# The order of the two halves' feed-forward layers around the second per-position attention: half 0 first, half 1 between the relays

## The reference, cut to what matters

```python
x = _layernorm(x + _L0_attn_ref(x, ...))   # per token: 32 heads attend to each other's 16 dims
x = _layernorm(x + _L0_ffn_ref(x, ...))    # three dense layers with +-1 weights, relu between them
x = _layernorm(x + _L1_attn_ref(x, ...))   # rotary, causal attention in a window of 128 tokens, 32 heads
x = _layernorm(x + _L1_ffn_ref(x, ...))    # a shared expert and the best 2 of 16 experts
```

## Time and profile before

| | |
|---|---|
| median of 3 runs | 777.63 us (777.32 to 779.89) |
| the profiled execution's own time | 780.3 us |
| its span, first to last instruction | 778.5 us |
| busy in the span | PE 83%, PEld 65%, DVE 53%, ACT 33%, POOL 27% |
| mean granted TensorE clock | 0.881 of 2.4 GHz |

### The profile page before, as it was taken

One profiled execution on the slowest core, in us unless ns is written; L12 is line 12 of the kernel. 1 busy time (PEld: TensorE's weight loads), 2 busy tenths in 40 slices (PEclk: granted clock), 3 DMA queues, 4 the chain that ended last, 5 costly groups with the idle time before them and its releaser, 6 DMA issues.

```text
span 778.5 us, 16447 instructions
## 1 busy us (share of the span) xinstructions
PE 643.4 (83%) x6644; PEld 502.8 (65%) x6644; DVE 412.6 (53%) x1155; ACT 253.2 (33%) x412; POOL 208.4 (27%) x305
## 2 busy tenths in 40 slices
PE   3998998864878687698998989596579979999984
PEld 3886877753756565476675766474347868887761
DVE  3445454478556375574776748462547224332354
ACT  4243001733437223232443334254321012221213
POOL 4000000462010115343544445245103621110061
PEclk9997998767889997698999989675789989999997
DMA  8920002131100752725537254602002939998455
GB/s 301 384 91 4 3 3 88 32 86 30 48 0 26 191 132 46 152 83 83 133 48 151 81 86 128 129 4 83 1 0 89 370 109 404 393 417 326 177 166 184
DMA packets 45786, 102.40 MB, mean 132 GB/s; under 512 B 11088, under 2 KB 15312, under 8 KB 44176
## 3 DMA queue, kind: packets, MB, share of 16 engines
q1 hardware_dynamic: 28528, 62.73, 22.6%
q0 software_dynamic: 12720, 30.50, 17.4%
q10 hardware_dynamic: 4464, 8.13, 2.8%
HBM read 63.77 MB, written 35.13 MB: 127 GB/s over the span
## 4 chain that ended last, share of the span: by engine, by line
PE 56%; DMA 12%; DVE 11%; issue 7%; ACT 6%; POOL 6%; SPq 1%; POOLq 0%; ACTq 0%; DVEq 0%
PE bank L317 15%; PE bank L353 10%; PE bank L526 10%; ACT FP L1487 3%; PE bank L594 3%; DVE FP L923 3%; DMA slots_out<-FP 3%; PE bank L609 3%; DMA QS<-QS 2%; PE bank L581 2%; POOL slots_in L1819 2%; DMA QS<-slots_out 2%; POOL FP L1831 2%; PE bank L729 2%; DVE W L923 2%
## 5 line engine op out<-in xcount | busy, mean ns | idle before, releaser
L1487 ACT ACTIVATE FP<-bank 128x512 f32<-128x512 f32 (+1 forms) x246 | 140.8, 612 | 335.2 <-PE bank L594 133.7
L1216 DVE CUSTOM_DVE_ANT_0 kraw<-bank,maskb 128x256 bf16<-128x256 f32 (+1 forms) x256 | 88.5, 401 | 63.9 <-PE bank L581 63.9
L526 PE MATMUL bank<-W,XR 128*128 128x512 f32 x384 | 116.1, 450 | 0.1
L317 PE MATMUL bank<-FP 128*128 128x128 f32 x558 | 89.3, 315 | 1.6 <-ACT FP L1487 1.6
L526 PEld LDWEIGHTS bank<-W,XR 128*128 128x128 f32 x384 | 78.5, 216 | 18.1 <-DVE XR L923 0.7
L353 PE MATMUL bank<-W,XR 128*128 128x512 f32 x288 | 82.0, 432 | 4.8 <-DVE W L923 4.8
L1782 POOL TENSOR_SCALAR_AFFINE_SELECT FP<-FP 128x512 f32<-128x512 f32 x64 | 41.3, 669 | 114.3 <-ACT FP L1487 114.3
L353 PEld LDWEIGHTS bank<-W,XR 128*128 128x128 f32 x288 | 60.9, 235 | 14.2 <-DVE W L923 5.2
L317 PEld LDWEIGHTS bank<-FP 128*128 128x128 f32 x558 | 67.0, 196 | 3.7 <-issue 2.1
L317 PE MATMUL bank<-RP,W 128*128 128x512 f32 x224 | 54.9, 402 | 4.3 <-DVE FP L923 2.2
L317 PEld LDWEIGHTS bank<-RP,W 128*128 128x128 f32 x224 | 42.8, 193 | 14.7 <-issue 4.4
(11 more groups left out here) (162 smaller groups left out, 1029.5 us busy)
## 6 DMA issues: line engine op xcount, KB each, us to landing
FP<-in_experts_dram SPq DMA_DIRECT2D x31, 768.0 KB, 6.7
slots_out<-QS SPq DMA_DIRECT2D x48, 256.0 KB, 2.6
FP<-slots_in POOLq DMA_DIRECT2D x31, 256.0 KB, 6.5
slots_out<-FP ACTq DMA_DIRECT2D x31, 256.0 KB, 7.2
slots_in<-RP SPq DMA_DIRECT2D x7, 1024.0 KB, 9.0
RP<-slots_out POOLq DMA_DIRECT2D x16, 384.0 KB, 5.8
QS<-slots_out POOLq DMA_DIRECT2D x10, 384.0 KB, 8.9
FP<-in_shared_dram SPq DMA_DIRECT2D x4, 768.0 KB, 8.3
```

Of the source, the lines that this page charges most:

```text
L317: mm = nc.tensor.matmul(bank, lhs, rhs, start=(n == 0), stop=(n == len(terms) - 1))
L526: mm = nc.tensor.matmul(b[:, :], *terms[n], start=(n == 0), stop=(n == len(terms) - 1))
L1216: ins = nc.vector.tensor_tensor_reduce(masked[:, 2 * (f % 2) + m, 0:n], b[:, m, :], maskb[:, m0:m0 + n], 1.0, -BIG, ALU.add, ALU.max, hmax ...
L1487: return nc.scalar.activation(o, i, func, **kw)
```

## The change

On PE half 0's first hidden layer moves into steps c = 6 and 7 of the second core, ahead of `values_by_four(6)` and `(7)`. Its second layer and last layer follow with half 1's context transposes in front or between; tile 0's projections (key, query) come right behind, ahead of all of half 1's FFN; half 1's FFN is laid between tile 0's and tile 1's rotations and projections; its four `last_layer` calls move into the loop's pass i = -1. In step c = 0 half 0's normalisation moves from DVE (`normalise`) to DVE's `rates` and ACT's `normalise`. `ffn_out` gives tile 0's statistics by themselves, so tile 0's root, rates and normalisation have a batch of their own. These buffers become separate ones: `h1[0]`, `hf`, tile 0's x2 (`x2T`); the stack semaphores become two for each kind, by the parity of the tile. SP's load of the output weights (`ao`) goes behind tile 1's relays; ACT's split of them from step (-1, 3) to (0, 6), and POOL's subtraction for them from (0, 1) to (1, 0). The diff, cut to its core:

```diff
-        h1 = [RP[:, 0:4096].rearrange("p (a c n) -> p a c n", a=2, c=DC),
+        h1 = [QS[:, 0:4096].rearrange("p (a c n) -> p a c n", a=2, c=DC),
...
-        hf = FP[:, 16512:17536].rearrange("p (b n) -> p b n", b=2)
+        hf = [FP[:, a:a + 1024].rearrange("p (b n) -> p b n", b=2) for a in (14336, 16512)]
...
+        x2T = [QS[:, 0:1024].rearrange("p (a c n) -> p a c n", a=2, c=DC)] + [XT2[:, 0]] * (T - 1)
+        coT = XT2[:, 1]
...
                 if AHEAD <= c < AHEAD + G:
                     turn_x1(c - AHEAD)
+                elif c >= AHEAD + G:
+                    hidden(0, 0, *range(2 * (c - AHEAD - G), 2 * (c - AHEAD - G) + 2))
                 values_by_four(c)
...
-            hidden(0, 0, 0)
             contexts(1, 0, 1)
-            hidden(0, 0, 1)
-            contexts(1, 2)
-            hidden(0, 0, 2)
-            contexts(1, 3)
-            hidden(0, 0, 3)
-            hidden(0, 1, *range(DC))
+            hidden(0, 1, 0)
+            contexts(1, 2, 3)
+            hidden(0, 1, 1, 2, 3)
+            last_layer(0, 0, 1, 2)
+            turn_x(0)
+            last_layer(0, 3)
+            project2(0, 1)
             turn_x1(G)
             turn_x1(G + 1)
-            last_layer(0, 0, 1)
+            project2(0, 0)
             turn_x1(G + 2)
             turn_x1(G + 3)
-            last_layer(0, 2, 3)
-            hidden(1, 0, 0, 1, 2)
-            turn_x(0)
+            turn_rotated(0, 1)
+            hidden(1, 0, 0, 1)
+            turn_rotated(0, 0)
+            hidden(1, 0, 2)
+            turn_x(1)
             hidden(1, 0, 3)
-            project2(0, 1)
-            project2(0, 0)
+            project2(0, 2)
+            project2(1, 1)
             hidden(1, 1, 0)
-            turn_rotated(0, 1)
-            hidden(1, 1, 1)
-            turn_rotated(0, 0)
-            project2(0, 2)
-            hidden(1, 1, 2, 3)
-            turn_x(1)
-            last_layer(1, 0)
-            project2(1, 1)
+            project2(1, 0)
+            turn_rotated(1, 1)
+            hidden(1, 1, 1, 2)
+            turn_rotated(1, 0)
+            hidden(1, 1, 3)
...
                     if (i, s) == (-1, 0):
-                        project2(1, 0)
-                        turn_rotated(1, 1)
+                        project2(1, 2)
+                    if i == -1 and s in (1, 3, 4, 5):
+                        last_layer(1, (1, 3, 4, 5).index(s))
                     if (i, s) == (-1, 2):
-                        project2(1, 2)
-                        turn_rotated(1, 0)
-                    if i == -1 and s in (1, 3, 4):
-                        last_layer(1, (1, 3, 4).index(s) + 1)
-                    if (i, s) == (-1, 3):
                         turn_x(2)
...
-                if t == 0:
+                if t == 1:
                     A.filled(sp, ("hidden", 1, 1, DC - 1))
+                    sp.wait_ge(stack_in[0][1], 32)
                     load_raw(3, ao)
...
-                    first_stats(0)
+                    first_stats(0, *range(G))
                 turn_weights(c)
                 if c >= 1:
                     contexts_by_four(c - 1)
                 if c == 0:
-                    normalise(slice(0, G), 0)
+                    rates(slice(0, G), 0)
                 if AHEAD <= c < AHEAD + G:
                     low_xt(("x1", c - AHEAD), tile_parts(c - AHEAD))
-                if 2 <= c < 6:
                     low_piece(2 * c - 4)
                     low_piece(2 * c - 3)
+            hidden_low(0, 0, 0, 1)
...
-            add_contexts(1, 0)
-            hidden_low(0, 0, 0)
-            add_contexts(1, 1)
-            hidden_low(0, 0, 1)
-            add_contexts(1, 2)
-            hidden_low(0, 0, 2)
-            add_contexts(1, 3)
-            hidden_low(0, 0, 3)
-            first_stats(1)
+            hidden_low(0, 0, 2, 3)
+            add_contexts(1, 0, 1)
             conn_weights(2)
-            hidden_low(0, 1, 0, 1)
+            add_contexts(1, 2, 3)
+            for o in range(DC):
+                hidden_low(0, 1, o)
+                first_stats(1, o)
             rates(slice(G, T), 1)
-            hidden_low(0, 1, 2, 3)
+            ffn_out(0, 0)
+            rates(slice(0, 1), 2)
+            ffn_out(0, 1)
+            low_dense(("x2", 0), xa[0][1], xa[0][0])
+            ffn_out(0, 2, 3)
+            rates(slice(1, G), 3)
             low_x1(G, G + 1)
-            ffn_out(0, 0, 1)
+            rotate(0, 1)
+            rope_sum(0, 1)
             low_x1(G + 2, G + 3)
-            ffn_out(0, 2, 3)
-            rates(slice(0, G), 2)
-            hidden_low(1, 0, 0, 1, 2)
-            low_dense(("x2", 0), xa[1], xa[0])
-            hidden_low(1, 0, 3)
+            parts_low(0, 1)
+            rotate(0, 0)
+            rope_sum(0, 0)
+            hidden_low(1, 0, 0)
+            parts_low(0, 0)
+            hidden_low(1, 0, 1)
             for m in range(8, 12):
                 low_piece(m)
-            rotate(0, 1)
-            rope_sum(0, 1)
-            rotate(0, 0)
-            hidden_low(1, 1, 0)
-            parts_low(0, 1)
-            rope_sum(0, 0)
-            hidden_low(1, 1, 1)
-            parts_low(0, 0)
-            hidden_low(1, 1, 2, 3)
-            low_dense(("x2", 1), xa[1], xa[0])
+            low_dense(("x2", 1), xa[1][1], xa[1][0])
+            hidden_low(1, 0, 2, 3)
             rotate(1, 1)
             rope_sum(1, 1)
+            hidden_low(1, 1, 0)
+            parts_low(1, 1)
+            rotate(1, 0)
+            rope_sum(1, 0)
+            hidden_low(1, 1, 1, 2)
+            parts_low(1, 0)
+            hidden_low(1, 1, 3)
...
-                    if i == -1 and s in (0, 2, 4, 5):
-                        ffn_out(1, (0, 2, 4, 5).index(s))
-                    if (i, s) == (-1, 0):
-                        parts_low(1, 1)
-                    if (i, s) == (-1, 1):
-                        rotate(1, 0)
-                        rope_sum(1, 0)
-                    if (i, s) == (-1, 2):
-                        parts_low(1, 0)
+                    if i == -1 and s in (2, 4, 5, 6):
+                        ffn_out(1, (2, 4, 5, 6).index(s))
                     if s == 5 and r < T:
                         maxima_out(r, 0)
                     if (i, s) == (-1, 6):
-                        rates(slice(G, T), 3)
+                        rates(slice(G, T), 4)
...
-            for c in range(1, NCH):
+            exponentials(1, 1)
+            s.wait_ge(offset_ready, 1)
+            for t in range(G):
+                normalise(t)
+            for c in range(2, NCH):
                 exponentials(1, c)
                 if AHEAD <= c < AHEAD + G:
                     high_xt(("x1", c - AHEAD), XT[:, 0, :, (c - AHEAD) * P:(c - AHEAD + 1) * P])
-                if 2 <= c < 6:
                     high_piece(2 * c - 4)
                     high_piece(2 * c - 3)
-
-
-            def hidden_out(g, layer, *which):
-                dst = (h1, h2)[layer][g]
-                for o in which:
-                    n = (2 * g + layer) * DC + o
-                    b = A.take(s, ("hidden", g, layer, o))
-                    if n >= 2:
-                        s.wait_ge(h_ready, n - 1)
-                    act(dst[:, 0, o, :], b[:, :], ACT.Relu, scale=scales[:, layer:layer + 1]).then_inc(act_step, 1)
-                    act(hf[:, o % 2, :], b[:, :], ACT.Relu, scale=scales[:, layer:layer + 1]).then_inc(A.free, 1)
+            hidden_out(0, 0, *range(DC))
...
-            hidden_out(0, 0, *range(DC))
-            hidden_out(0, 1, 0, 1)
+            hidden_out(0, 1, *range(DC))
+            high_piece(8)
+            high_piece(9)
             roots(slice(G, T), 1)
-            hidden_out(0, 1, 2, 3)
-            s.wait_ge(offset_ready, 1)
-            normalise(G)
+            s.wait_ge(offset_ready, 2)
             for t in range(G, T):
-                if t + 1 < T:
-                    normalise(t + 1)
+                normalise(t)
+            roots(slice(0, 1), 2)
+            s.wait_ge(offset_ready, 3)
+            normalise(0)
+            high_dense(("x2", 0), x2T[0][:, 0])
+            roots(slice(1, G), 3)
+            for t in (G, G + 1):
                 high_xt(("x1", t), x1T[1][:, 0, :, t % G * P:(t % G + 1) * P])
-            hidden_out(1, 0, 0, 1)
-            roots(slice(0, G), 2)
-            s.wait_ge(offset_ready, 2)
-            normalise(0)
+            s.wait_ge(offset_ready, 4)
+            normalise(1)
+            for t in (G + 2, G + 3):
+                high_xt(("x1", t), x1T[1][:, 0, :, t % G * P:(t % G + 1) * P])
+            parts_out_high(0, 1)
+            hidden_out(1, 0, 0)
+            high_piece(10)
+            high_piece(11)
+            hidden_out(1, 0, 1)
+            parts_out_high(0, 0)
             hidden_out(1, 0, 2)
-            high_dense(("x2", 0), XT2[:, 0, 0])
+            high_dense(("x2", 1), x2T[1][:, 0])
             hidden_out(1, 0, 3)
-            for m in range(8, 12):
-                high_piece(m)
```

(39 more changed lines are left out.)

76 lines of the change are left out of this document (37 added, 39 removed).

## The result

| | before | changed kernel |
|---|---|---|
| median of 4 runs each | 778.76 us (777.32 to 783.21) | 756.28 us (753.38 to 760.62) |
| the profiled execution | 780.3 us, span 778.5, granted clock 0.881 | 753.38 us, span 751.5, granted clock 0.898 |
| ratio, 95% interval | | 0.9707 (0.9637 to 0.9776) |

The change gains 22.5 us between the medians; the prediction was 18.6, to 759.0. The changed kernel was timed twice more later: 754.52 (6 runs, ratio 0.9734, 0.9672 to 0.9796) and 760.95 (6 runs, ratio 0.963, 0.955 to 0.971). The ratios leave out executions more than 1.5% above the fastest of their kernel, which of the last six leaves 744.9 and 750.5. The figure that doesn't swim with the rest of the kernel is a distance inside it. I take two marks: the **root**, ACT's `std<-mv` of half 0 right ahead of the second core, at 165.37 before, and `key_scores(0, 0, 0)`, at 297.72.

What follows compares the result with a forecast made beforehand. DVE bounds the kernel up to 186, then PE with holes, waiting for tiles 0 and 1's relays. `key_scores(0, 0, 0)` moves from 297.72 to 279.1, all behind shifts rigidly: 777.63 - 18.6 = 759.0 us, range 754.5 to 768.

Steps and rivals of the forecast that it cites:

- sign of error: Behind the front: the forecast is wrong if the time from `key_scores(0, 0, 0)` to the end grows.
- (e): Front of the kernel: more gain, with no cold piece and a maxima transfer of 2.5; gain 22, 755.5; chance 0.05.
- Second core: Up to the end of `hidden(0, 1)`: four products start earlier, cold products and a hole go; 215.0 to 205.9, gain 9.1 us.
- From there to the pass i = -1: From the end of `hidden(0, 1)` to `row_scores(0, 0)`: PE's work 42.4 and holes 5.8, at 254.1 instead of 270.92.
- a hole of 1.3: At `turn_x(0)`: PE waits 1.3 us, as ACT's work lasts to 214.9 and `last_layer(0, 2)` covers only to 213.6.
- the one cold piece that I had priced at 1.9: Behind the 2.2 us hole for `hidden_low(0, 1, 3)`: products at half clock, plus 1.9 us, bounded between 0 and 3.8.
- The pass i = -1: From `row_scores(0, 0)` to `row_scores(1, 0)`: DVE's list of 16.9 us bounds it, with waits; 21.2 us in all, to 275.3.
- The maxima transfer: Ahead of `key_scores(0, 0, 0)`: POOL's fill until 271.2, issue 1.2, transfer 3.5, landing taken as 277.2; the load beside it costs 0.
- (a): Second core to pass i = 0: some forty handoffs eat half the gain, leaving 9 to 14; 764 to 769; chance 0.20.
- (b): Pass i = 0: the maxima transfer or the relays bound it; gain 11.5 to 15, 763 to 766; chance 0.09.
- (c): Behind the front: the shift isn't rigid, because something later is fixed in time; 774 to 777.6; chance 0.05.
- (d): From 186 to 275: PE's clock falls to half; a loss beyond 20.5 us of such work, 782 at 25; chance 0.04.

Runs made afterwards that it cites:

- experiment 5: Changed kernel without SP's wait for tile 1's query relay ahead of the load of the output weights; a single execution took 767.41 us.
- experiment 4: Changed kernel with tile 1's query projection and both its rotations' turns back in the pass i = -1; 758.59 us, ratio 0.977.
- Experiments 2: Kernel before, with only half 0's first hidden layer in c = 6, 7 and the context transposes behind it; 775.17 us, ratio 0.9927.
- experiment 3: Changed kernel with half 0's first hidden layer back behind the second core; 769.23 us, ratio 0.9864.

## Why the prediction was right, and where it was off

**The place and the mechanism held.** Two groups of products stand ahead of each of the last two value products; the first 48-row matmul waits for no DMA; the pass i = 0 is held by DVE, then for 0.28 us by the maxima transfer. The time from the mark to the end was 480.8 before and 477.4, 479.7 and 488.4 in three executions of the changed kernel: what I had named as a sign of error, that it grows, stands in the last of them. Of its 11.0 us 3.5 are in the five passes and 7.6 behind them, in instructions that the change leaves as they were, at a lower granted clock (below).

**Why the time was in the range.** The gain of 21.7 us (22.5 by the medians) lies above the 15 to 21 that the forecast gave a chance of 0.57; it is next to rival (e), 22 us and 755.5, which had 0.05. The measured 756.28 is within 754.5 to 768 because the range took (e) in, not because the sum met it, and the errors below partly cancel.

**Second core: gain 9.1 forecast, 7.7 measured.** The move from DVE to ACT gave 0.7 us instead of 0.4 (root to the start of the last x1 remainder 20.61 before, 19.88 after). The term that was mis-sized is "two products of `hidden(0, 0)` at the full clock's 1.86 to 1.9": they took 5.47 us instead of 3.8. I had concluded from the granted clock of 1.00 in 176 to 186 that PE would stay there at this load. It did not: 0.84 in the same stretch after, with more work in it, and 0.50 from 185 to 188. Of ten executions of kernels that have this piece in this order, three ran it at full clock (3.87 to 3.91) and seven did not (5.40 to 5.51).

**From there to the pass i = -1: 50.1 us forecast, 47.8 measured.** PE's idle time is 4.5 us instead of 5.8. The difference is `turn_x(0)`, for which I had a hole of 1.3: ACT finished tile 0 at 214.08, and `last_layer(0, 2)` ended at 214.75, since it was 1.5 us late itself. This is the one cold piece that I had priced at 1.9: it came in this place with 7.34 - 5.85 = 1.5, and hid the hole that I had added beside it. The two terms were not independent, and the sum took both. The remaining 1.0 is work: PE is busy for 43.3 us, the cold piece included, against 42.4 + 1.9.

**The pass i = -1: 21.2 forecast, 19.8 measured.** DVE's list was the bound as said, 15.3 us of work where I had summed 16.9, and 3.7 us of waits where I had 4.3.

**The maxima transfer: 1.9 after the row scores forecast, 1.1 measured.** POOL's fill ended 3.3 us before `row_scores(1, 0)`, where I had 4.1. From there to the transfer's landing it took 0.55 + 3.79 = 4.3 us, where I had 6.0: the issue 1.2 and the transfer's 3.5, but 277.2 as the sum where these make 275.9. The transfer's 3.79 is near the 3.5 of the earlier trace rows although 2 us of it are the load beside it (experiment 5), which I had put at 0: in the kernel before, the same transfer ran beside the read of tile 1's relay and took 3.91, so its row held a cost of this kind already.

Together (+1.4) - 2.3 - 1.4 - 0.8 = -3.1 us: the gain is 21.7 and not 18.6. The terms that were mis-sized are small, and three of the four lean to one side; in two of these the sum stands above its own terms (42.4 for PE's work, listed as 42.0, and 277.2 for 275.9).

**The rivals.** (a), handoffs eat half, fell: between the marks the changed kernel was faster than the sum, so the forty handoffs cost nothing beyond the holes in it. (b), relays or transfer bound the pass 0, fell; the transfer did pay for the load beside it, but 0.28 us of that reached PE, and experiment 4 shows that even with tile 1's relay waited for the mark doesn't move by more than 1 us. (c), the shift isn't rigid, fell as well: tile 2's relay read, behind the mark, moved by 21.0 of the 21.7 us. (d), the clock, was right in direction and small: 3.2 us of cold pieces in the front (1.7 + 1.5), against 20.5 needed; a third of 2.4 us, tile 2's key projection, stands behind the mark. Against the kernel before the clock gave time back, 4.1 us of busy time in the front. (e), more gain, is what came, though with two cold pieces and a transfer of 3.8 us, not with none and 2.5: its number was met, not its reason.

**What is open.** Experiments 2 and 3 split the gain in two; within the larger part no run separates tile 0's early projections from the late `last_layer` calls of half 1. The 21.7 us rest on one trace of the kernel before. The medians' 22.5 and the marks' 21.7 agree within the noise; whether the later passes get anything from the change can't be said at this noise.

## What to carry to other kernels

Measure a reordering between two instructions of the trace that enclose it, since one execution's total says 26.9 where the change is 21.7. A wait that disappears is not a gain by itself: with tile 1's relay late again a wait of 4.2 us came back and the mark moved by 1 us at most; count instead by when the next work behind the wait can start. And where a hole and a cold piece are next to each other, price them together: the cold piece delays the work and covers the hole.

## What the runs showed of the hardware

The same pass of the same kernel, in two executions (stretches, columns as in the earlier trace rows; first the changed kernel, then its third execution):

```profile
295.00:329.00 34.00, 27.05 (x223) 20.80 (x218) 22.91 (x93) 13.15 (x22) 17.91 (x23) 0.75 0.49 104
329.00:360.00 31.00, 28.03 (x298) 21.40 (x298) 22.20 (x91) 12.49 (x23) 14.58 (x25) 0.94 0.50 98
```

```profile
295.00:329.00 34.00, 27.16 (x234) 21.04 (x234) 22.87 (x93) 13.15 (x22) 18.05 (x23) 0.76 0.49 103
329.00:363.00 34.00, 29.28 (x303) 22.58 (x298) 22.41 (x91) 12.49 (x23) 14.69 (x25) 0.90 0.45 93
```

The second pass takes 31 us with a granted clock of 0.94 or 34 us with 0.90, with DVE's, ACT's and POOL's work equal to 0.2 us; the first is alike in both. PE is busy for 1.25 us longer in the 34 us and idle for 1.75 longer, so the clock goes with the length but isn't shown to make all of it. Over the traces of the study the five passes from tile 2's relay read to tile 7's took 30.5 to 35.2 us each. The time differs in three places: ahead of the root (161.6 to 168.9 in the study), in these five passes together (163.0, 163.2 and 166.5 in three executions of the changed kernel) and in the layers behind them (260.9, 263.7 and 268.5 us, at a granted clock of 0.88, 0.88 and 0.85, PE busy for 223.9, 227.4 and 232.6). Together this is the size of the spread of 744.9 to 765.3 us among sixteen executions of the changed kernel.

A piece behind the same wait does not always meet the same clock. Where the first two products of `hidden(0, 0)` ran cold, as in the changed kernel, the granted clock was 1.00 from 182 to 184 and 0.50 from 185 to 188; in the kernel of experiment 4, one of the three that ran them at full clock, it was 0.50 from 178 to 180, under the last `scores_by_four` ahead of the piece, and 1.00 from 182 to 187, with the same wait of 0.5 us in front of the piece. No run sets which of the two comes.

And a hole does not fix what follows it: behind the same wait of 2.08 us the 24 matmuls of `last_layer(0, 0..2)` took 7.33 to 7.37 us in all ten executions with the changed front, 5.78 in the kernel of experiment 3 (granted clock 0.50 in 209 to 211 in the one, 1.00 in 216 to 226 in the other). What PE did before differs there: with half 0's first layer behind the second core it had run a cold piece at 195 (8 matmuls in 2.98 us), and another behind a hole of 2.13 us at 206.7 (8 in 3.24). Why the clock falls behind one hole and not behind the other no run separates.
